# Attention with keys on partitions in a graph layer's twelve attention passes

## The chip, the cores and the metric

The kernel runs on one core of one Trainium2 chip. The metric is the device time in microseconds of one execution; the median of three runs is given. TensorE is written PE in the profile, VectorE DVE, ScalarE ACT, GpSimd POOL, SyncE SP.

## What is computed

A layer over 1250 nodes of 512 features: a graph convolution and a linear attention (not touched), then a block with three attentions of 8 heads, then an MLP. The three attentions are what the change is about:

```python
def attend(q, k, v):           # heads of 64 columns, 1250 tokens
    att = softmax(q @ k.T * 64 ** -0.5)
    return att @ v
spatial  = attend(xs @ Wq, xs @ Wk, xs @ Wv) @ Wo        # xs: one normed input
temporal = xt + attend_causal(xt @ Wq, ...) @ Wp         # keys after the query are masked
fused    = attend(spatial @ Cq, temporal @ Ck, temporal @ Cv) @ Co
```

Weights of the first two are those of an expert that a router picks. All is float32 in and out.

## The kernel before

Float32 products are made of two parts: hi (rounded to fp32r) and lo (the rest), and a product of three matmuls, hi by hi, hi by lo, lo by hi. The 8 heads of an attention are taken two at a time, so there are 12 passes (n = 0 to 11): 0 to 3 spatial, 4 to 7 temporal (causal), 8 to 11 the crossed one. In a pass two heads of 64 features lie on 128 partitions. The 1250 tokens are 10 tiles of 125 (TOK).

Steps of a pass, each written out in a list (STEPS, and lists for ScalarE and VectorE made from it):
- "u": q and k for both heads, features on partitions, 3 pieces of 418 columns each, 12 matmuls a piece (`unit`, L1892). ScalarE makes hi (L1124), VectorE lo (L1493).
- "v": values with tokens on partitions, 120 matmuls of 128 columns (`values`, L1930); ScalarE and VectorE write v_tok (L1163, L1549).
- "s": scores of one tile of queries against up to 500 keys, for the two heads in the two halves of the array (6 matmuls of 64 rows, L1951, L1959, L1961). VectorE takes them out of PSUM negated and scaled, with the row's minimum (L1516); ScalarE makes the exponential of a whole row and its sum (L1144), VectorE the reciprocal (L1529, one or two elements), GpSimd multiplies the whole row by it (L940).
- "t": a batch. Four 125x125 pieces of the probabilities are turned by TensorE (L1976); ScalarE rounds them to pt_hi (L1181), VectorE makes pt_lo (L1581).
- "p": 4 matmuls of 250 columns add the batch's part of the output to one bank (L1992). After the last batch of a unit (a pair of tiles and a head) ScalarE and VectorE write feat (L1152, L1539).

There are 50 batches in an unmasked pass and 30 in a causal one, 520 in all. The next pass's "u" and "v" stand near the end of a pass. In pass 1 a fold joins two weight matrices (`fold`, L1909). Between passes 7 and 8 GpSimd splits the planes of the temporal output and TensorE projects them (`project`, L2005), with a chain of VectorE and ScalarE behind each of the four projections (L1557, L1560, L1188, L1562). GpSimd also splits all weights into hi and lo (L848, L850); SyncE loads them in the order of use.

## Time and profile before

| what | value |
|---|---|
| median of 3 runs | 2180.38 us (2180.33 to 2619.19) |
| profiled execution | 2188.32 us |
| its span, first to last instruction | 2186.5 us |
| mean granted TensorE clock | 0.941 |
| TensorE, VectorE, ScalarE, GpSimd busy | 86%, 60%, 38%, 28% |
| attention stage, first "u" to last output | 515.4 to 1885.9 us |

Busy time is the union of an engine's instructions. TensorE's matmuls overlap in the profile, so what one costs is read from the distance of the starts, not from its duration. The granted clock is 1.0 at full speed and 0.5 at half.

### The profile page before, as it was taken

What the parts mean: (1) busy time and instruction counts of PE and PEld (TensorE: products, weight loads), DVE (VectorE), ACT (ScalarE), POOL (GpSimd) and SP (SyncE); (2) the same over time, 40 slices, a digit from 0 to 9 for tenths busy, and PEclk for the clock granted to TensorE, in tenths of its full rate; (3) what the DMA queues carried; (4) which work ended last, traced back from release to release, by engine and by line L of the source; (5) the groups of instructions that cost most, each with busy time, mean ns of one, the idle gap of its engine ahead of it and who ended that gap; (6) DMA issues with size and microseconds to landing.
All of it is one profiled execution on the core that took longest, in us unless ns stands there. A gap on an engine that the chain in (4) does not pass through costs nothing.

```text
span 2186.5 us, 35324 instructions
## 1 busy us (share of the span) xinstructions
PE 1885.5 (86%) x11839; PEld 1604.6 (73%) x11839; DVE 1302.4 (60%) x3667; ACT 828.7 (38%) x1490; POOL 602.7 (28%) x575
## 2 busy tenths in 40 slices
PE   1999999866898998989888887888989898876998
PEld 1687577655787886979777776777878786776886
DVE  6576577766676546575645546457676767552332
ACT  0223111022565545565544435246565655320000
POOL 2210011001324315141322213513231315546330
PEclk9999999957999998999989999899999999997999
DMA  3001000023000000020000000000000001002101
GB/s 97 30 6 44 6 25 15 1 104 119 15 1 25 20 30 15 18 92 1 16 1 15 11 6 16 18 6 12 1 16 1 16 1 72 29 28 68 39 29 47
DMA packets 24417, 60.83 MB, mean 28 GB/s; under 512 B 2522, under 2 KB 4790, under 8 KB 23373
## 3 DMA queue, kind: packets, MB, share of 16 engines
q1 hardware_dynamic: 24260, 58.74, 8.0%
q8 instruction: 98, 1.61, 0.3%
q14 instruction: 59, 0.48, 0.1%
HBM read 44.87 MB, written 13.86 MB: 27 GB/s over the span
## 4 chain that ended last, share of the span: by engine, by line
PE 56%; issue 14%; POOL 13%; DVE 10%; ACT 4%; DMA 1%; DVEq 1%; SPq 1%; POOLq 0%; ACTq 0%
PE ps L1892 7%; POOL probs L940 7%; PE ps L1992 7%; PE ps L2041 6%; PE ps L1976 6%; PE ps L1716 5%; PE ps L1930 4%; PE ps L1796 3%; PE ps L2070 3%; PE ps L1828 3%; PE ps L1951 3%; DVE probs L1516 2%; PE ps L1729 1%; DVE pt_lo L1581 1%; ACT pt_hi L1181 1%
## 5 line engine op out<-in xcount | busy, mean ns | idle before, releaser
L940 POOL TENSOR_SCALAR probs<-probs,stats 125x1250 f32<-125x1250 f32 (+4 forms) x240 | 280.8, 1180 | 926.0 <-DVE stats L1529 926.0
L1581 DVE TENSOR_TENSOR pt_lo<-ps,pt_hi 125x500 fp32r<-125x500 f32 x520 | 351.3, 677 | 186.2 <-ACT pt_hi L1181 181.2
L1181 ACT ACTIVATE pt_hi<-ps 125x500 fp32r<-125x500 f32 x520 | 304.8, 588 | 368.0 <-PE ps L1976 363.8
L1976 PE MATMUL ps<-ident,probs 125*125 125x125 f32 x2080 | 332.3, 286 | 87.3 <-POOL probs L940 87.3
L1992 PE MATMUL ps<-pt_hi,v_tok 125*128 125x250 f32 x1040 | 319.0, 328 | 55.5 <-DVE feat L1539 55.3
L1976 PEld LDWEIGHTS ps<-ident,probs 125*125 125x125 f32 x2080 | 285.7, 198 | 103.0 <-POOL probs L940 96.3
L1516 DVE TENSOR_SCALAR_CACHE_REDUCE probs<-ps 125x416 f32<-125x416 f32 (+5 forms) x624 | 340.6, 585 | 16.2 <-PE ps L1961 15.3
L1992 PEld LDWEIGHTS ps<-pt_hi,v_tok 125*128 125x128 f32 x1040 | 204.0, 196 | 139.4 <-DVE pt_lo L1581 77.5
L1144 ACT ACTIVATE probs<-probs,stats 125x1250 f32<-125x1250 f32 (+4 forms) x240 | 286.1, 1193 | 15.1 <-DVE stats L1521 15.1
L1992 PE MATMUL ps<-pt_lo,v_tok 125*128 125x250 f32 x1040 | 274.9, 286 | 0.0
L1992 PEld LDWEIGHTS ps<-pt_lo,v_tok 125*128 125x128 f32 x1040 | 205.5, 198 | 0.4
L1375 DVE TENSOR_SCALAR onehot<-iota_h,win_key,key_t 125x320 f16 x453 | 169.9, 375 | 0.5 <-issue 0.3
L1374 DVE TENSOR_SCALAR onehot<-iota_h,low_t 125x125 f16 x453 | 126.8, 280 | 61.8 <-PE ps L1828 31.8
L1951 PE MATMUL ps<-k_hi,q_hi 64*125 64x416 f32 (+5 forms) x624 | 146.9, 467 | 8.7 <-DVE k_lo L1493 5.8
L1930 PE MATMUL ps<-w_hi,xa_hi 128*125 128x128 f32 x480 | 131.3, 274 | 0.0
L1930 PE MATMUL ps<-w_lo,xa_hi 128*125 128x128 f32 x480 | 130.9, 273 | 0.0
L1930 PE MATMUL ps<-w_hi,xa_lo 128*125 128x128 f32 x480 | 130.8, 272 | 0.0
L1959 PE MATMUL ps<-k_hi,q_lo 64*125 64x416 f32 (+5 forms) x624 | 118.4, 375 | 0.0
L1961 PE MATMUL ps<-k_lo,q_hi 64*125 64x416 f32 (+5 forms) x624 | 114.7, 363 | 0.0
L1828 PE MATMUL ps<-onehot 125*125 x453 | 86.8, 312 | 17.8 <-DVE onehot L1375 17.3
L1796 PE MATMUL ps<-near_rows,adj 125*125 125x257 f32 (+1 forms) x400 | 94.5, 388 | 2.4 <-issue 2.1
L1951 PEld LDWEIGHTS ps<-k_hi,q_hi 64*125 64x125 f32 x624 | 59.8, 188 | 49.4 <-DVE k_lo L1493 7.6
(341 smaller groups left out, 3494.8 us busy)
## 6 DMA issues: line engine op xcount, KB each, us to landing
w_raw<-in_w_mlp SPq DMA_DIRECT2D x32, 256.0 KB, 2.6
w_raw<-in_w_gps SPq DMA_DIRECT2D x16, 256.0 KB, 2.6
w_raw<-in_w_tp SPq DMA_DIRECT2D x16, 256.0 KB, 2.6
w_raw<-in_w_sp SPq DMA_DIRECT2D x12, 256.0 KB, 5.4
w_raw<-in_w_cr SPq DMA_DIRECT2D x12, 256.0 KB, 2.6
d_xt<-xb_hi SPq DMA_DIRECT2D x1, 2508.0 KB, 9.3
d_xt<-xb_lo SPq DMA_DIRECT2D x1, 2508.0 KB, 14.9
xa_hi<-d_xt SPq DMA_DIRECT2D x1, 2508.0 KB, 9.6
```

The costliest lines, as they stand in the source:

```text
L940: pool.tensor_scalar(p, p, stats[:, slot, 7:8], 1.0, ALU.mult, ALU.mult).then_inc(s_prob, 1)
L1144: act.activation(p, p, ACT.Exp, scale=-1.0, bias=st[:, least:least + 1], accum_out=st[:, 4:5]).then_inc(s_exp, 1)
L1181: act.activation(pt_hi[:, (BASE_B[n] + m) % PT, :], ps[0:TOK, ring_bank(ring_of(n, m)), 0:4 * TOK], ACT.Copy)\
L1375: ins = dve.tensor_scalar(row[:, ET:ET + DH], iota_h[0:ET, :], win_key[0:ET, bass.ds(w, 1)], key, ALU.add, ALU.is_equal)
L1516: dve.tensor_scalar(probs[:, slot + h, first:first + w], ps[0:TOK, bank + h, 0:w], -SCALE, None, ALU.mult, ALU.min, accum_out=stats[:, slo ...
L1581: dve.tensor_tensor(pt_lo[:, slot, :], ps[0:TOK, ring_bank(ring_of(n, m)), 0:4 * TOK], f32(pt_hi[:, slot, :]), ALU.subtract).then_inc(s_pt ...
L1796: ins = pe.matmul(ps[0:TOK, bank + h, 0:257 - h], adj[t // 4][:, x, cols], near_rows[:, x, h, 0:257 - h], start=(x == 0), stop=(x == NT - 1))
L1892: ins = pe.matmul(ps[:, x % 4, 0:NP], w[:, k % 3, 128 * c:128 * c + 128], src[:, c, NP * p:NP * p + NP], start=(c == 0 and y == 0), stop=( ...
L1930: ins = pe.matmul(ps[0:TOK, ring_bank(r), 128 * t:128 * t + 128], x[:, c, (t0 + t) * TOK:(t0 + t + 1) * TOK], w[:, k % 3, 128 * c:128 * c ...
L1951: pe.matmul(ps[0:TOK, bank + h, 0:w], q_hi[r, tile], k_hi[r, first:first + w], start=True, stop=False)
L1976: ins = pe.transpose(ps[0:TOK, ring_bank(r), x * TOK:(x + 1) * TOK], probs[:, slot, kt * TOK:(kt + 1) * TOK], ident[0:TOK, 0:TOK])
L1992: ins = pe.matmul(ps[:, OUT_BANK, 0:2 * TOK], v_tok[:, kt, y % 2, :], part[:, slot, 2 * TOK * x:2 * TOK * (x + 1)], start=(kt == 0 and par ...
```

## The change

Scores are computed with keys on partitions and queries in the columns, so that the exponentials are already what the products need and nothing is turned. A step (n, i, h, b) is a pair of query tiles i, a head h and a pair of key tiles b; there are again 520. The parts:
- The row maximum must be known before. Approximate scores hi by hi are made in the old orientation, 64 rows, for both heads into banks 5 and 6 (task M), reduced by VectorE to a column, turned by TensorE (task R), and written negated by ScalarE into row 64 or 0 of q_row, whose partner in k_rest holds ones. The score matmul subtracts it.
- A score takes two matmuls of 250 columns for each key tile: k_both holds the head's hi on both halves, q_both has q's hi and lo; k_rest has k's lo and the ones, q_row q's hi and the row. Keys and queries are therefore written twice by ScalarE and in halves by VectorE.
- ScalarE writes the exponential to p_raw, GpSimd its fp32r part p_hi, VectorE p_lo.
- The values are linear like the keys, three pieces of 418 columns, and are turned by TensorE 64 columns at a time (task T). v_ones has the values' hi and 64 columns of ones, so that the products sum the probabilities too; a third matmul adds the values' lo part (v_rest): 6 matmuls in a step.
- At the end of a unit VectorE makes the reciprocal of the 64x250 sums and multiplies the output with it. Two output banks take turns.
- q is made in five pieces of 250 columns, in three ring slots. K, V, Q, M, R, T and the fold F are side tasks, put into steps by a planner with the costs in COST and a due step for each; each engine follows the same plan. Weights have a slot for each role; loads, splits and planes are put to steps too. Of the planes split between passes 7 and 8, two are split in pass 7 and the last by ScalarE and VectorE.

```diff
+STEP = [(n, i, h, b) for n in range(PASSES) for i in range(5) for h in range(2) for b in range(blocks_in(n, i))]
+STEP_NO = {s: g for g, s in enumerate(STEP)}
...
+COST = {"K": 2.3, "V": 2.3, "Q": 1.4, "M": 0.3, "R": 0.2, "T": 0.3, "F": 3.0}
...
+def tensor_steps():
+
+    steps = []
+    for first, end in ((0, FIRST[8, 0]), (FIRST[8, 0], len(STEP))):
+        if first:
+            steps.append(("J",))
+        steps += OPENING[STEP[first][0]] + [("S", first + x) for x in range(LEAD)]
+        for g in range(first, end):
+            if g + LEAD < end:
+                steps.append(("S", g + LEAD))
+            steps += SIDE[g] + [("P", g)]
...
+            def p_high(g):
+
+                pool.wait_ge(s_exp, g + 1)
+                if g >= PR:
+                    pool.wait_ge(s_pv, g - PR + 1)
+                pool.tensor_copy(p_hi[:, g % PR, :], p_raw[:, g % PR, :]).then_inc(s_p_hi, 1)
...
+            for g in range(LEAD):
+                p_high(g)
+            for g in range(len(STEP)):
+                if g + LEAD < len(STEP) and not FIRST[8, 0] - LEAD <= g < FIRST[8, 0]:
+                    p_high(g + LEAD)
...
+            def key_copy(n, p):
+
+                bias, b0 = BIAS[n // 4]
+                col, bank = b0 + n % 4, BANKS["K", n, p][0]
+                cols = slice(NP * p, NP * p + NP)
+                for h, r in enumerate(HALF):
+                    ins = act.activation(k_both[h][HALF[1 - h], n % 2, cols], ps[r, bank, 0:NP], ACT.Identity, bias=bias[r, col:col + 1])
+                ins.then_inc(s_k_both, 1)
...
+            def row_in(n, i):
+
+                bank = BANKS["R", n, i][0]
+                act.wait_ge(s_max_row, 5 * n + i + 1)
+                for h, r in ((0, 64), (1, 0)):
+                    ins = act.activation(q_row[h][r:r + 1, ring(n, i), :], ps[32 * h:32 * h + 1, bank, 0:2 * TOK], ACT.Copy, scale=-1.0)
+                ins.then_inc(s_max_in, 1)
...
+            def exponent(g):
+
+                act.wait_ge(s_score, g + 1)
+                if g >= PR:
+                    act.wait_ge(s_p_lo, g - PR + 1)
+                act.activation(p_raw[:, g % PR, :], ps[0:TOK, g % 3, 0:4 * TOK], ACT.Exp, scale=SCALE).then_inc(s_exp, 1)
...
-            def shift(n, u, j):
-
-                width, pieces = PLAN[n // 4][u]
-                if j == 0 and u >= 4:
-                    dve.wait_ge(s_pt, BASE_B[n] + last_batch(n, u // 2 * 2 - 3) + 1)
-                if j == 0 and u < 4 and n:
-                    dve.wait_ge(s_pt, BASE_B[n - 1] + last_batch(n - 1, u // 2 * 2 + 7) + 1)
-                bank, first, w = pieces[j]
-                dve.wait_ge(s_score, pieces_to(n, u) + j + 1)
-                slot = (20 * n + 2 * u) % PROBS
-                for h in range(2):
-                    dve.tensor_scalar(probs[:, slot + h, first:first + w], ps[0:TOK, bank + h, 0:w], -SCALE, None, ALU.mult,
-                                      ALU.min, accum_out=stats[:, slot + h, j:j + 1]).then_inc(s_taken, 1)
...
+            def maximum(n, i, y, j):
+
+                first, w = key_pieces(n, i)[j]
+                part = max_part[:, ring(n, i), :, :, :]
+                dve.wait_ge(s_max, MAX_NO["M", n, i, y, j])
+                dve.tensor_reduce(part[:, y, :, j], ps[0:TOK, 5:7, 0:w], AX.X, ALU.max).then_inc(s_max_part, 1)
...
+            def p_low(g):
+
+                dve.wait_ge(s_p_hi, g + 1)
+                if g >= PR:
+                    dve.wait_ge(s_pv, g - PR + 1)
+                dve.tensor_tensor(p_lo[:, g % PR, :], p_raw[:, g % PR, :], f32(p_hi[:, g % PR, :]), ALU.subtract).then_inc(s_p_lo, 1)
...
+            def unit_out(g):
+
+                n, i, h, _ = STEP[g]
+                u = unit_of(g)
+                dve.wait_ge(s_pv, g + 1)
+                dve.reciprocal(share[:, u % 2, :], ps[64:128, 3 + u % 2, 0:2 * TOK]).then_inc(s_share, 1)
+                dve.wait_ge(s_share, u + 1)
+                dve.tensor_tensor(feat[HALF[h], n % 4, 2 * TOK * i:2 * TOK * (i + 1)], ps[0:64, 3 + u % 2, 0:2 * TOK], share[:, u % 2, :],
+                                  ALU.mult).then_inc(s_o, 1)
...
+                for g in range(first, end):
+                    for what, *at in SIDE[g]:
+                        if what == "M":
+                            maximum(*at)
+                    if g > first and ends(g - 1):
+                        unit_out(g - 1)
+                    if g + LEAD < end:
+                        p_low(g + LEAD)
+                    if g > first:
+                        for task in SIDE[g - 1]:
+                            last_out(task)
+                    for what, *at in SIDE[g]:
+                        if what == "T":
+                            value_lo(*at)
...
+            def maximum(n, i, y, j):
+
+                first, w = key_pieces(n, i)[j]
+                tile = slice(TOK * y, TOK * y + TOK)
+                rows = [slice(ROW * h, ROW * h + ROW) for h in range(2)]
+                masked = CAUSAL[n // 4] and j == len(key_pieces(n, i)) - 1
+                left(("M", n, i, y, j))
+                pe.wait_ge(s_q_hi, 5 * n + i + 1)
+                pe.wait_ge(s_k_both, 3 * n + 3)
+                for h, r in enumerate(rows):
+                    ins = pe.matmul(ps[0:TOK, 5 + h, 0:w], q_both[h][r, ring(n, i), tile], k_both[h][r, n % 2, first:first + w],
+                                    start=True, stop=True)
...
+            def max_rows(n, i):
+
+                bank = BANKS["R", n, i][0]
+                left(("R", n, i))
+                pe.wait_ge(s_max_col, 5 * n + i + 1)
+                for y in range(2):
+                    ins = pe.transpose(ps[0:33, bank, TOK * y:TOK * y + TOK], max_col[:, ring(n, i), y, :], ident[0:TOK, 0:TOK])
+                ins.then_inc(s_max_row, 1)
...
+            def score(g):
+
+                n, i, h, b = STEP[g]
+                left(("S", g))
+                if h == 0 and b == 0:
+                    pe.wait_ge(s_max_in, 5 * n + i + 1)
+                    pe.wait_ge(s_q_lo, 5 * n + i + 1)
+                    if i == 0:
+                        pe.wait_ge(s_k_lo, 3 * n + 3)
+                if g == FIRST[4, 0]:
+                    pe.wait_ge(s_turned, 2)
+                rest = slice(0, 65) if h == 0 else slice(0, 128)
+                for x in range(2):
+                    tile = slice((2 * b + x) * TOK, (2 * b + x + 1) * TOK)
+                    to = ps[0:TOK, g % 3, 2 * TOK * x:2 * TOK * (x + 1)]
+                    pe.matmul(to, k_both[h][:, n % 2, tile], q_both[h][:, ring(n, i), :], start=True, stop=False)
+                    if CAUSAL[n // 4] and b == i:
+                        pe.matmul(to, identb[0:TOK, 0:TOK], mask_turned[0:TOK, TOK * (1 - x):TOK * (3 - x)], start=False, stop=False,
+                                  skip_group_check=True)
+                    ins = pe.matmul(to, k_rest[h][rest, n % 2, tile], q_row[h][rest, ring(n, i), :], start=False, stop=True)
...
-            def turned(n, m, y, b):
-
-                r = ring_of(n, m)
-                if b == 0:
-                    pe.wait_ge(s_prob, 20 * n + 4 * (y // 2) + y % 2 + 3)
-                if m < 3:
-                    pe.wait_ge(s_v_lo, 3 * n + m + 1)
-                else:
-                    pe.wait_ge(s_pt_lo, BASE_B[n] + m - 2)
-                for x in range(4):
-                    kt, u = 2 * b + x // 2, y // 2 * 2 + x % 2
-                    slot = (20 * n + 2 * u + y % 2) % PROBS
-                    ins = pe.transpose(ps[0:TOK, ring_bank(r), x * TOK:(x + 1) * TOK], probs[:, slot, kt * TOK:(kt + 1) * TOK],
-                                       ident[0:TOK, 0:TOK])
...
+            def product(g):
+
+                n, i, h, b = STEP[g]
+                bank = 3 + unit_of(g) % 2
+                pe.wait_ge(s_p_lo, g + 1)
+                left(("P", g))
+                for z in range(3):
+                    if first_use(n, h, z) == g or z == 1 and first_use(n, h, 1) == g:
+                        pe.wait_ge(s_turn_lo, TURN_NO["T", n, h, z])
                 for x in range(2):
-                    kt = 2 * b + x
-                    for part in (pt_hi, pt_lo):
-                        ins = pe.matmul(ps[:, OUT_BANK, 0:2 * TOK], v_tok[:, kt, y % 2, :],
-                                        part[:, slot, 2 * TOK * x:2 * TOK * (x + 1)],
-                                        start=(kt == 0 and part is pt_hi), stop=(kt == last and part is pt_lo))
+                    kt, cols, last = 2 * b + x, slice(2 * TOK * x, 2 * TOK * (x + 1)), b == blocks_in(n, i) - 1 and x == 1
+                    pe.matmul(ps[:, bank, 0:2 * TOK], v_ones[:, kt, h, :], p_hi[:, g % PR, cols], start=(b == 0 and x == 0), stop=False)
+                    pe.matmul(ps[:, bank, 0:2 * TOK], v_ones[:, kt, h, :], p_lo[:, g % PR, cols], start=False, stop=last)
+                    ins = pe.matmul(ps[0:64, bank, 0:2 * TOK], v_rest[:, kt, h, :], p_hi[:, g % PR, cols], start=False, stop=last,
+                                    skip_group_check=True)
```

## Rows read from the trace of the kernel before

**Rows 1.** The page: busy time of each engine, its share of the span, instructions

```profile
PE 1885.5 (86%) x11839; PEld 1604.6 (73%) x11839; DVE 1302.4 (60%) x3667; ACT 828.7 (38%) x1490; POOL 602.7 (28%) x575
```

**Rows 2.** Windows: busy time of each engine (instructions), TensorE's granted clock, DMA share, GB/s

```profile
515.40:1885.90 1370.50, 1211.16 (x8729) 1055.51 (x8730) 846.22 (x2334) 701.46 (x1276) 437.45 (x418) 0.95 0.06 21
515.40:556.10 40.70, 35.04 (x235) 32.16 (x235) 13.82 (x45) 9.38 (x18) 3.89 (x3) 0.92 0.37 147
668.50:805.50 137.00, 122.91 (x854) 106.32 (x852) 79.03 (x225) 67.02 (x118) 45.02 (x42) 0.95 0.10 30
1134.30:1229.40 95.10, 79.04 (x581) 69.57 (x581) 51.62 (x145) 44.51 (x92) 23.26 (x27) 0.93 0.03 9
1385.60:1458.40 72.80, 61.51 (x377) 57.22 (x376) 33.23 (x57) 14.06 (x22) 24.42 (x26) 0.99 0.05 15
1569.90:1681.40 111.50, 103.83 (x775) 90.15 (x773) 76.87 (x218) 64.16 (x114) 31.64 (x26) 0.98 0.03 8
```

**Rows 3.** Timeline of TensorE, one step of pass 8: start, us, instruction, count

```profile
1543.64 0.60 PE L1976 MATMUL ps<-ident,probs 125*125 125x125 f32 x4
1544.17 0.45 PE L1951 MATMUL ps<-k_hi,q_hi 64*125 64x418 f32 x2
...
1544.94 0.38 PE L1992 MATMUL ps<-pt_hi,v_tok 125*128 125x250 f32 x1
1545.16 0.28 PE L1992 MATMUL ps<-pt_lo,v_tok 125*128 125x250 f32 x1
...
1545.51 0.60 PE L1976 MATMUL ps<-ident,probs 125*125 125x125 f32 x4
```

**Rows 4.** Timeline of TensorE, inside a linear of keys, then of values

```profile
1539.24 0.35 PE L1892 MATMUL ps<-xa_lo,w_hi 128*128 128x418 f32 x1
1539.43 0.35 PE L1892 MATMUL ps<-xa_hi,w_lo 128*128 128x418 f32 x1
...
1560.58 0.27 PE L1930 MATMUL ps<-w_hi,xa_hi 128*125 128x128 f32 x1
1560.69 0.27 PE L1930 MATMUL ps<-w_lo,xa_hi 128*125 128x128 f32 x1
```

**Rows 5.** Waits of the whole span: who waited for whom, us, times, longest

```profile
PE ps L1976 <- POOL probs L940: 87.3, 39, 5.1
...
PE ps L1992 <- DVE feat L1539: 55.3, 72, 1.6
```

**Rows 6.** Lines by form, VectorE: busy us, mean ns, idle before

```profile
L1581 DVE TENSOR_TENSOR pt_lo<-ps,pt_hi 125x500 fp32r<-125x500 f32 x520 | 351.3, 677 | 186.2 <-ACT pt_hi L1181 181.2 <-issue 0.2
...
L1539 DVE SCALAR_TENSOR_TENSOR feat<-ps,tp_vecs,o_half 64x250 f32<-64x250 f32 x40 | 18.9, 473 | 43.9 <-ACT o_half L1152 43.4
...
L1549 DVE TENSOR_TENSOR v_tok<-ps,v_tok 125x256 fp32r<-125x256 f32 x48 | 17.8, 419 | 61.2 <-ACT v_tok L1163 61.1
...
L1493 DVE SCALAR_TENSOR_TENSOR k_lo<-ps,sp_vecs,k_hi 128x418 fp32r<-128x418 f32 x12 | 7.8, 653 | 19.7 <-ACT k_hi L1124 19.7
```

**Rows 7.** Lines by form, VectorE: a maximum and the two longest reciprocals

```profile
L1413 DVE TENSOR_REDUCE key_st<-mix_k 128x1 f32<-128x1250 f32 x4 | 5.8, 1455 | 13.8 <-ACT mix_k L1050 10.6 <-issue 2.1 <-ACT mix_v L1053 1.1
...
L1257 DVE RECIPROCAL ln_r<-ln_r 125x10 f32<-125x10 f32 x3 | 0.6, 216 | 2.2 <-ACT ln_r L1018 2.2
...
L1622 DVE RECIPROCAL end_r<-end_r 125x4 f32<-125x4 f32 x2 | 0.3, 160 | 0.0
```

**Rows 8.** Timeline: one subtraction of VectorE twice, and GpSimd beside the first

```profile
1418.86 1.85 DVE L1562 TENSOR_TENSOR xa_lo<-proj_tmp,xa_hi 128x1254 fp32r<-128x1254 f32 x1 [1.32 <-ACT xa_hi L1188]
...
1425.15 1.47 DVE L1562 TENSOR_TENSOR xa_lo<-proj_tmp,xa_hi 128x1254 fp32r<-128x1254 f32 x1 [1.31 <-ACT xa_hi L1188]
...
1418.09 1.30 POOL L850 TENSOR_TENSOR w_lo<-w_raw,w_hi 128x512 fp32r<-128x512 f32 x1
```

**Rows 9.** Lines by form, GpSimd's cast and ScalarE's reading of a 500-column bank

```profile
L848 POOL CAST w_hi<-w_raw 128x512 fp32r<-128x512 f32 x44 | 29.8, 678 | 108.9 <-DMA w_raw<-in_w_sp 43.3 <-PE ps L1729 29.6 <-DMA w_raw<-in_w_gps 23.6
...
L1181 ACT ACTIVATE pt_hi<-ps 125x500 fp32r<-125x500 f32 x520 | 304.8, 588 | 368.0 <-PE ps L1976 363.8
```

More of the change, by code:

```diff
@@ L1588, in _ @@
+                for task in SIDE[end - 1]:
+                    last_out(task)
+                unit_out(end - 1)
             for p in range(3):
@@ L1896, in fold @@
             def fold(x):
-                bank = (6 + x) % 4
+                bank = BANKS["F", x][0]
+                left(("F", x))
                 if x == 0:
```

1073 lines of the change are left out of this document (578 added, 495 removed).

## The prediction

> **What bounds the kernel now.** I read the page's busy shares first [rows 1]: TensorE is busy for 86% of the span, VectorE for 60%. Then the windows, with their edges at the first transposition (L1976) of a pass [rows 2]. The attention stage lasts 1370.5 us of the 2186.5, and TensorE is busy for 1211 of them, VectorE for 846. A pass without the causal mask takes 111.5 us (VectorE busy for 76.9), a causal one 95.1 (51.6), pass 1 with the fold 137.0, and from the end of pass 7 to the start of pass 8 72.8 go by.
>
> Pitches, not durations, give TensorE's cost, since its matmuls overlap. A product with 250 columns costs 0.117 us and the first after scores 0.22; four transpositions 0.53; three pairs of score matmuls 0.77, or 0.26 a pair [rows 3]. A linear with 418 columns costs 0.19, one with 128 columns 0.11 [rows 4]. An unmasked pass then holds 72 x 0.19 + 120 x 0.11 = 26.9 for q, k and v, 30 steps with scores of 1.87 (56.1) and 20 without, of 0.9 (1.87 less the scores and the 0.2 around them; 18): 101 us of work in 111.5. TensorE bounds these passes and gets 0.91 of the time. Its long waits are for the divided rows (87.3 us) and for the one output bank (55.3) [rows 5].
>
> **The change, TensorE.** It loses the 2080 transpositions of probabilities and two thirds of the 64-row score matmuls. Per unmasked pass after: k and v 72 x 0.19 = 13.7; q in 60 matmuls of 250 columns, 7.0; 20 turns of values and 10 of maxima at 0.11, 3.3; 30 pairs for the maxima at 0.26 and 0.1 for the row change behind each, 10.8; 50 steps of 4 score and 6 product matmuls, 500 x 0.117 = 58.5. Sum 93.3 against 101. The same sum for a causal pass (30 steps, 18 pairs, masks some 5) is 70.4. With 14 for the fold and 27 for the projection (144 x 0.19) TensorE has 8 x 93.3 + 4 x 70.4 + 41 = 1069 us.
>
> **The change, VectorE.** Here it adds more than it removes. 624 shifts with their minima go, 520 subtractions stay, and four things come.
> - The low part p_lo, 520 x 0.677 = 352 us [rows 6]. It now reads two tiles of SBUF.
> - The maxima. A reduction of 1250 elements took 1.455 us [rows 7]. A tensor_tensor grows by 1.06 ns per element (0.677 at 500, 0.419 at 256) [rows 6]; with 1.04 for a reduction, 833 elements in two banks cost 1.455 - 0.434 = 1.02. 240 unmasked pieces make 245 us. The 18 of a causal pass hold 15000 elements, 15.6 + 18 x 0.155 = 18.4, times four 74. With 60 short closing reductions at 0.16 (the shortest kind of row [rows 7]), 329.
> - The division of an output tile, 120 times a reciprocal of 64x250 and a product. The product is at most the 0.473 of today's last step over the same shape [rows 6], 0.45 taken. The reciprocal isn't shown at this size. From 4 to 10 elements it grows by 56 ns, 9.3 ns each [rows 7]; carried on, that is 0.216 + 240 x 0.0093 = 2.45 us. The low end, if only the part above a fixed 0.155 counts, is 6.1 ns each, 1.68. I take 2.1, between them: 120 x 2.55 = 306 us.
> - The halves of keys and queries: 72 x 0.653 + 120 x 0.473 = 104, and 72 low parts of values at about 0.38, 27 [rows 6].
>
> Sum 1118 us, 101.7 per unmasked pass and 75.9 per causal one. VectorE is above TensorE (93.3 and 70.4) in both, so the bound moves to it. The Trainium skill, VectorE: DVE Perf Modes, First, the fixed hardware budget, says that the reciprocal is an iterative divide with a repeat count of 8. At 0.96 GHz that would be an estimated 8.3 ns per element, 2.2 us for 250, and 12 us more in all than I count; the trace's 6.1 to 9.3 ns has it inside.
>
> **Its neighbours.** p_lo has two inputs in SBUF, and GpSimd reads SBUF beside it. The same kind of subtraction took 1.47 us alone and 1.85 with GpSimd's 1.30 us operation begun 0.77 us before it: it waited for the rest, some 0.4 [rows 8]. The Trainium skill, SBUF — State Buffer, Who interferes with whom, states this as an exclusive lock of a shared port; the trace agrees. GpSimd's new cast of 500 elements costs about 0.66 (0.678 for 512 [rows 9]), 520 times, beside the splits of weights. In a kernel that VectorE bounds, a cast starts about 2 us after the p_lo that let its products go (products 0.7, scores 0.47, the exponential, handovers), when the next p_lo is mostly over; I count only the splits, 30 us. If every p_lo met half a cast it would be 172.
>
> ScalarE: 50 exponentials at 0.59 and 51 short readings at up to 0.61 are at most 60 us per pass [rows 9], hidden. GpSimd: 33 for casts and some 11 for splits and planes, hidden. From a score to p_lo is 0.59 + 0.66 + 0.68 and three handovers, some 2.3 us; TensorE has two steps (at least 2.3, with side work 3.7) for it, so this loop doesn't bind. The two output banks take the wait of 55 us away; the wait for divided rows goes with the division on rows. The weights' DMAs move with the steps; a split stands some 12 steps (over 20 us) before its use, so SyncE's queue, in the same order, costs nothing; if that cover were gone, one late load would cost its few us, once.
>
> **Edges.** The opening drops from 40.7 us [rows 2] to about 28: six linears of 2.3 (12 x 0.19) and two of 1.4 are 16.6, and behind them run the last maximum, its turn, the row, the first score, exponential, cast and subtraction, with ScalarE's second copies in front, some 11. GpSimd's new memsets lie beside it. From pass 7 to 8: 3 us for the last plane, 9 until the first projection is complete, 25 of VectorE's chain of four projections, 28 of opening, 65 against 72.8. The last division adds 3 at the end. The extra time of the fold in pass 1 (137.0 against 111.5 [rows 2]) is in the stage's total of today; after, TensorE's 14 us lie under VectorE.
>
> **Sum.** VectorE's 1118 + 30, less some 32 that lie in the two openings, 1116. How well an engine in this chain of in-order lists is kept at work I take from today's bound, 0.91: 1226. With 28 + 65 + 3 the stage takes 1322 in place of 1370.5, 48.5 less. The span goes to 2138, the profiled execution (1.8 above its span) to 2140, and with its 8 us over the median, 2188.3 against 2180.4, the median to 2131.
>
> **Rivals.**
> - A: the reciprocal runs at one element per cycle at this size. For it: the 0.16 us of the small ones is all start-up. Against it: the 56 ns between 4 and 10 elements. VectorE falls by 120 x 1.65 = 198 to 920, TensorE bounds: (1069 - 67 for the projection and the openings) / 0.91 = 1101, plus 96; 173 less, 2007.
> - B, slower: lumps of the two engines don't hide each other. A linear holds TensorE for 2.3 us, and the maximum behind it in TensorE's list is first in VectorE's next step; a turn of values shares its bank with the next maximum, so VectorE waits one round (0.6) for it. With 132 linears at w and 72 turns at 0.6 in place of the 0.91, the stage is 96 + 1116 + 43 + 132 w; it passes today's from w = 0.9. At 1.7 (2.3 less a backlog of 0.6) it is 1479, and the time 2289. For it: 11 linears in 30 to 50 steps; against: the plan spaces them, and VectorE's division gives it a backlog.
> - C: p_lo meets a cast each time, 142 more, 156 with the 0.91, 2287. For it: the lock seen above. Against: the phase worked out above.
> - D: VectorE is kept at 0.97 of the time, since it does nothing else but wait for what is ready two steps ahead: 1116 / 0.97 + 96 = 1247, 124 less, 2056.
> - E: the new order starves at the short units at the start of a causal pass, so that these gain nothing and the forecast loses its 4 x 10 us: 2175.
>
> **How the numbers follow.** The forecast, with 0.88 to 0.95 of VectorE's time, 2080 to 2175: 0.40. A 0.13, B 0.18 (half of it between 2175 and 2225), C 0.06, D 0.15, E 0.08. The range reaches from A's time to the middle of B: 2005 to 2235. A measurement of this kernel tells 2% from no change. Faster than 2137: A, D and somewhat over half of the forecast, 0.51. Slower than 2224: half of B and most of C, 0.15. The same: 0.34.
>
> **What would show it.** VectorE's busy share in the stage should rise from 0.62 to 0.85 or more with TensorE's below it; the reciprocal's row should read 1.7 to 2.45 us; p_lo near 0.7 on the mean (1.0 for C); TensorE's main wait should be for p_lo. Rows of VectorE waiting for maxima, over 100 us, would be B. If VectorE is under 0.8 and TensorE too, the forecast's 0.91 is the step that failed.

## The result and the profile after

The changed kernel takes 2398.26 us (median of 4 runs, 2383.86 to 2409.42), the kernel before 2184.39 beside it: a ratio of 1.098, with 95% interval [1.090, 1.106]. One of the four runs of the kernel before was in a slow state (2619.19 us); ratios are of the means of the others. The forecast was 2131, with a range of 2005 to 2235.

The page of the kernel after, busy time of each engine, and the groups of its costliest new lines (columns as in [rows 1] and [rows 6]):

```profile
PE 1986.5 (83%) x11351; PEld 1694.8 (71%) x11351; DVE 1549.7 (65%) x2752; ACT 732.5 (31%) x1361; POOL 689.5 (29%) x856
...
L986 POOL CAST p_hi<-p_raw 125x500 fp32r<-125x500 f32 x520 | 346.1, 668 | 1019.6 <-ACT p_raw L1273 940.1
L1686 DVE TENSOR_TENSOR p_lo<-p_raw,p_hi 125x500 fp32r<-125x500 f32 x520 | 379.6, 735 | 182.9 <-POOL p_hi L986 179.5
...
L1662 DVE TENSOR_REDUCE max_part<-ps 125x2 f32<-125x832 f32 (+5 forms) x312 | 319.3, 1023 | 172.0 <-PE ps L2133 136.5
...
L2133 PE MATMUL ps<-k_both_a,q_both_a 64*125 64x416 f32 (+5 forms) x312 | 155.6, 499 | 125.0 <-DVE max_part L1662 89.0
L1693 DVE RECIPROCAL share<-ps 64x250 f32<-64x250 f32 x120 | 206.7, 1722 | 19.7 <-PE ps L2197 16.1
```

VectorE has 247 us more to do than in [rows 1]. The forecast had some 300 more (1118 + 30 against 846 in the stage), and the sizes of the single instructions are near its own: p_lo 0.735 us (0.677 and 30 us for the port were counted), a maximum 1.02, a cast 0.67, a reciprocal 1.72 (2.1 taken, 1.68 its low end). The time is lost elsewhere.

Windows of the kernel after: the attention stage, its first opening, then a causal pass, pass 7 with the projection and opening behind it, and passes 8 and 9. They answer to [rows 2]; the edges are the first product of a pass here, and the first transposition there.

```profile
513.20:2075.60 1562.40, 1308.66 (x8232) 1143.88 (x8232) 1089.80 (x1416) 602.67 (x1143) 513.33 (x690) 0.89 0.06 18
513.20:556.20 43.00, 35.71 (x156) 30.78 (x157) 17.25 (x28) 17.39 (x34) 10.86 (x12) 0.74 0.29 120
...
1218.70:1317.70 99.00, 82.20 (x559) 72.61 (x558) 71.38 (x96) 41.72 (x82) 25.47 (x36) 0.93 0.03 9
1413.70:1563.30 149.60, 116.82 (x671) 103.78 (x671) 102.02 (x114) 45.96 (x84) 52.04 (x64) 0.86 0.05 13
1563.30:1694.90 131.60, 114.84 (x737) 99.24 (x735) 98.75 (x129) 54.76 (x103) 41.62 (x57) 0.92 0.03 9
1694.90:1831.60 136.70, 114.72 (x711) 99.83 (x710) 95.03 (x127) 52.80 (x101) 38.35 (x56) 0.86 0.03 7
```

The stage takes 1562.4 us in place of 1370.5, 192 of the 195.6 us that the spans differ by. Passes 8 and 9 take 132 and 137 in place of 111.5 each, a causal pass 99.0 in place of 95.1. VectorE is busy for 1089.8 / 1562.4 = 0.70 of the stage, TensorE for 0.84. Neither is full. Pass 7 is no exception. In the kernel before, the 72.8 us of [rows 2] follow a short pass 7, which holds no linears of a next pass:

```profile
1324.70:1385.60 60.90, 47.82 (x340) 40.63 (x341) 37.27 (x100) 33.91 (x72) 25.98 (x33) 0.86 0.05 14
```

Together they are 60.9 + 72.8 = 133.7 us before, and 149.6 after.

Waits over the whole span (who waited for whom, us, times, longest):

```profile
DVE p_lo L1686 <- POOL p_hi L986: 179.5, 122, 5.9
...
DVE max_part L1662 <- PE ps L2133: 136.5, 95, 4.1
...
PE ps L2133 <- DVE max_part L1662: 89.0, 67, 3.0
...
PE ps L2159 <- DVE max_part L1662: 40.0, 28, 4.8
DVE max_part L1662 <- PE ps L2139: 32.6, 23, 4.8
...
PE ps L2195 <- DVE p_lo L1686: 20.1, 22, 1.9
```

The two engines wait for each other: VectorE 169 us (136.5 + 32.6) for the maxima's matmuls, TensorE 129 us (89.0 for the next maxima, 40.0 for turns of values) for a reduction that lets it write banks 5 and 6 again. The waits of [rows 5] (87.3 for the divided rows, 55.3 for the output bank) are gone, and these stand in their place.

To compare runs I split TensorE's stage into three parts. From its rows in the trace I take each distance from one start to the next, less the wait in it, sorted by line and by the granted clock. A line's mean distance at full clock, times its count, is its work; what the same matmuls took beyond that at a granted clock of 0.5 (1.2 GHz) is the surplus; the waits are the third part. The split is good to some 10 us. Before: 1163 + 48 + 159 = 1370. After: 1176 + 132 + 252 = 1560. **So the change takes no work off TensorE (13 us more), adds 93 us of waits, and 84 us come from time at the lower clock.** Why the clock is lower for longer isn't shown, since no run changes the clock alone.

### The profile page after: what moved, and what is told of

Same layout as the page of the kernel before. It is cut to its first block, busy times and chain, and to the rows that moved or that the text cites. A ratio compares the mean times of both kernels' runs of the same rounds, so it can differ in the third digit from the quotient of the medians.

```text
span 2382.1 us, 34620 instructions
## 1 busy us (share of the span) xinstructions
PE 1986.5 (83%) x11351; PEld 1694.8 (71%) x11351; DVE 1549.7 (65%) x2752; ACT 732.5 (31%) x1361; POOL 689.5 (29%) x856
## 4 chain that ended last, share of the span: by engine, by line
PE 59%; DVE 24%; issue 6%; POOL 4%; ACT 3%; DMA 1%; DVEq 1%; SPq 1%; POOLq 0%; ACTq 0%
PE ps L2075 11%; DVE max_part L1662 7%; PE ps L2250 6%; DVE p_lo L1686 5%; DVE share L1693 5%; PE ps L1889 5%; PE ps L2195 4%; PE ps L2133 4%; PE ps L1969 3%; PE ps L2197 3%; PE ps L2196 3%; PE ps L2279 3%; PE ps L2177 3%; PE ps L2181 3%; PE ps L2001 3%
## 5 line engine op out<-in xcount | busy, mean ns | idle before, releaser
L986 POOL CAST p_hi<-p_raw 125x500 fp32r<-125x500 f32 x520 | 346.1, 668 | 1019.6 <-ACT p_raw L1273 940.1
L1686 DVE TENSOR_TENSOR p_lo<-p_raw,p_hi 125x500 fp32r<-125x500 f32 x520 | 379.6, 735 | 182.9 <-POOL p_hi L986 179.5
L1273 ACT ACTIVATE p_raw<-ps 125x500 f32<-125x500 f32 x520 | 304.7, 587 | 462.5 <-PE ps L2181 456.4
L1662 DVE TENSOR_REDUCE max_part<-ps 125x2 f32<-125x832 f32 (+5 forms) x312 | 319.3, 1023 | 172.0 <-PE ps L2133 136.5
L2195 PE MATMUL ps<-p_hi,v_ones 125*128 125x250 f32 x1040 | 339.9, 327 | 21.1 <-DVE p_lo L1686 20.1
L2196 PE MATMUL ps<-p_lo,v_ones 125*128 125x250 f32 x1040 | 304.8, 293 | 0.0
L2197 PE MATMUL ps<-p_hi,v_rest 125*64 125x250 f32 x1040 | 304.5, 293 | 0.0
L2195 PEld LDWEIGHTS ps<-p_hi,v_ones 125*128 125x128 f32 x1040 | 209.9, 202 | 71.3 <-issue 34.0
L1693 DVE RECIPROCAL share<-ps 64x250 f32<-64x250 f32 x120 | 206.7, 1722 | 19.7 <-PE ps L2197 16.1
L2196 PEld LDWEIGHTS ps<-p_lo,v_ones 125*128 125x128 f32 x1040 | 214.6, 206 | 0.4
L2181 PE MATMUL ps<-q_row_a,k_rest_a 65*125 65x250 f32 x520 | 146.8, 301 | 0.0
L2181 PE MATMUL ps<-q_row_b,k_rest_b 128*125 128x250 f32 x520 | 146.4, 301 | 0.0
```

What stands on the lines that cost most here:

```text
L986: pool.tensor_copy(p_hi[:, g % PR, :], p_raw[:, g % PR, :]).then_inc(s_p_hi, 1)
L1273: act.activation(p_raw[:, g % PR, :], ps[0:TOK, g % 3, 0:4 * TOK], ACT.Exp, scale=SCALE).then_inc(s_exp, 1)
L1662: dve.tensor_reduce(part[:, y, :, j], ps[0:TOK, 5:7, 0:w], AX.X, ALU.max).then_inc(s_max_part, 1)
L1686: dve.tensor_tensor(p_lo[:, g % PR, :], p_raw[:, g % PR, :], f32(p_hi[:, g % PR, :]), ALU.subtract).then_inc(s_p_lo, 1)
L1693: dve.reciprocal(share[:, u % 2, :], ps[64:128, 3 + u % 2, 0:2 * TOK]).then_inc(s_share, 1)
L2181: ins = pe.matmul(to, k_rest[h][rest, n % 2, tile], q_row[h][rest, ring(n, i), :], start=False, stop=True)
```

## The experiments

All are edits of the kernel after, and all ratios are to the kernel before. Stage and parts (us) are those of the profiled run. nodiv leaves out the division; shortmax and tinymax leave out the search for the row maximum. These three don't compute the layer, and only price a part.

| run | us | ratio, 95% interval | stage | work + surplus + waits |
|---|---|---|---|---|
| before | 2180 to 2190 | 1 | 1370 | 1163 + 48 + 159 |
| after | 2398 | 1.098 [1.090, 1.106] | 1562 | 1176 + 132 + 252 |
| lead3 | 2395 | 1.094 [1.088, 1.099] | 1573 | 1172 + 157 + 242 |
| nodiv | 2318 | 1.059 [1.055, 1.063] | 1494 | 1175 + 123 + 195 |
| shortmax | 2232 | 1.020 [1.014, 1.026] | 1402 | 1168 + 72 + 160 |
| moved3 | 2359 | 1.078 [1.075, 1.082] | 1527 | 1173 + 129 + 221 |
| fullrows2 | 2428 | 1.111 [1.109, 1.114] | 1605 | 1165 + 137 + 300 |
| splitmax | 2416 | 1.106 [1.103, 1.109] | 1597 | 1210 + 163 + 222 |
| turn7 | 2471 | 1.132 [1.129, 1.135] | 1646 | 1164 + 193 + 286 |
| best2 | 2371 | 1.086 [1.083, 1.090] | 1547 | 1153 + 131 + 261 |
| halves | 2515 | 1.149 [1.143, 1.155] | 1700 | 1178 + 201 + 319 |
| halvesmoved | 2463 | 1.126 [1.120, 1.132] | 1626 | 1179 + 151 + 294 |
| mfirst | 2484 | 1.135 [1.129, 1.141] | 1662 | 1182 + 218 + 259 |
| tinymax | 2219 | 1.015 [1.009, 1.020] | 1389 | 1121 + 89 + 177 |
| ring3 | 2329 | 1.066 [1.063, 1.069] | 1508 | 1197 + 118 + 191 |
| aligned | 2370 | 1.086 [1.083, 1.090] | 1549 | 1178 + 144 + 224 |
| alignring | 2278 | 1.042 [1.039, 1.046] | 1458 | 1194 + 95 + 167 |
| alignringmoved | 2230 | 1.021 [1.018, 1.024] | 1409 | 1186 + 75 + 145 |
| best3 | 2232 | 1.018 [1.013, 1.023] | 1404 | 1182 + 84 + 135 |
| best4 | 2234 | 1.020 [1.016, 1.024] | 1400 | 1171 + 72 + 155 |

**Is it the amount of VectorE's work, or the depth of the pipeline?** (lead3, nodiv, shortmax, moved3)

```diff
 lead3:   -LEAD = 2; PR = 3     +LEAD = 3; PR = 4     (p_lo lies over p_raw)
 nodiv:   -dve.reciprocal(share[:, u % 2, :], ps[64:128, 3 + u % 2, 0:2 * TOK])
          +dve.tensor_scalar(share[:, u % 2, :], ps[64:128, ...], 0.0, 0.01, ALU.mult, ALU.add)
 shortmax:-dve.tensor_reduce(part[:, y, :, j], ps[0:TOK, 5:7, 0:w], AX.X, ALU.max)
          +dve.tensor_reduce(part[:, y, :, j], ps[0:TOK, 5:7, 0:2], AX.X, ALU.max)
          and ACT.Exp with scale=0.001
 moved3:  act.activation(p_hi, p_raw, ACT.Copy); pool.tensor_tensor(p_lo, p_raw, p_hi, subtract); as lead3
```

> The scores run three steps ahead of the products in place of two, with four slots for the probabilities; the exponential and its low part share a buffer (the low part is written over it) so that they fit. No work is added or removed. Lumps (a long side task of one engine starves the other because only two steps of work are ready between them): the waits of VectorE for p_hi (180 us in the changed kernel) fall below 80 us, the time falls by 50 to 120 us, to 2280 to 2350. Work (VectorE's amount of work sets the time, whatever the order): no change beyond 1%, 2375 to 2420. Shared banks (TensorE held at a maximum until VectorE has reduced the one before, 131 us for maxima and turns): those waits stay, the time falls by less than 40.

> The reciprocal of the 64x250 sums is replaced by a tensor_scalar of the same shape that writes a constant, so the division is left out: 120 times 1.72 us become about 0.41, 157 us less of VectorE's work, in one lump per unit. Work: the time falls by 157 or more (157 / 0.7 = 224 at the share of the stage in which VectorE is busy now), to 2175 to 2240. Lumps: the lump at the end of a unit is one of several, the time falls by 60 to 130, to 2270 to 2340. Clock (TensorE's stalls cost above all by the half clock behind them): the granted clock, 0.899 now, rises by the same share as the waits fall, and the fall is more than the removed waits of TensorE.

> The maxima are made over two columns of each bank in place of all, and the exponential's scale is 0.001 so that it stays finite: the search for the row maximum is left out, all matmuls stay. 312 reductions fall from 1.02 us to about 0.17, 265 us less of VectorE's work, and banks 5 and 6 are free 0.85 us earlier after each. Work: the time falls by 265 or more, to below 2130. Shared banks: TensorE's 131 us of waits for the maxima go nearly away and VectorE's for TensorE's maxima stay; with the smaller work 200 to 300 less. Lumps of the linears alone: under 120 less, since the linears of 2.3 us stay.

> ScalarE writes p_hi (a second activation, SBUF to SBUF, 500 elements, about 0.6 us), GpSimd makes p_lo (a two-input subtraction of 500 elements, about 1.27 us, alone), VectorE has neither: 380 us less of VectorE's work, ScalarE 300 more, GpSimd 310 more. With three steps ahead, as in the run beside it. Work of VectorE: the stage would be set by TensorE (93 us of work per unmasked pass) or by ScalarE (50 x 1.2 + 30 = 90): 8 x 103 + 4 x 80 + 96 = 1240 for the stage, the time 2060 to 2130, below the kernel before. Lumps: 2150 to 2280, with the waits of TensorE for p_lo growing, since the way from score to product is 2.9 us long.

VectorE's wait for p_hi in lead3, windows of the stage in nodiv and in shortmax, and three waits of moved3:

```profile
DVE p_lo L1687 <- POOL p_hi L987: 175.8, 120, 5.9
```

```profile
514.50:2008.80 1494.30, 1298.37 (x8232) 1136.84 (x8232) 945.47 (x1416) 603.36 (x1144) 508.04 (x688) 0.90 0.06 19
```

```profile
514.50:1916.70 1402.20, 1240.29 (x8232) 1092.33 (x8232) 833.48 (x1415) 603.44 (x1143) 516.26 (x689) 0.94 0.06 20
```

```profile
DVE max_part L1667 <- PE ps L2135: 314.7, 192, 6.3
...
PE ps L2135 <- DVE max_part L1667: 67.0, 51, 2.6
...
PE ps L2161 <- DVE max_part L1667: 37.8, 28, 3.2
```

The third step of lead changes nothing: the time stays, and so does VectorE's wait for p_hi, 176 us where the theory of lumps wanted under 80. Taking 144 us off VectorE by leaving out the reciprocal gives back 68 of the stage, 256 us off the reductions give 160, and 347 us of p_lo moved elsewhere give 36 (46 against lead3, which has the same lead). What a microsecond on VectorE is worth depends on where it stands: 0.6 in a reduction, 0.5 in a division, 0.1 in the low parts. With VectorE busy for half the stage (moved3), TensorE still waits 105 us for reductions. The amount isn't the bound; the reduction between two maxima is on the path. The expectations did worse than this reading: in time, nodiv's 80 us lie in the range for lumps, but shortmax's 166 and moved3's 39 lie in none of their ranges.

**Is it TensorE's row pairs, the pair of banks, or the turns in them?** (fullrows2, splitmax, turn7, best2)

```diff
 fullrows2: -ins = pe.matmul(..., q_both[h][r, ring(n, i), tile], k_both[h][r, n % 2, ...])
            +ins = pe.matmul(..., q_both[h][:, ring(n, i), tile], k_both[h][:, n % 2, ...])
 splitmax:  +for h in range(2): wait for s_max of this head; reduce ps[0:TOK, 5 + h, 0:w]; s_max_part + 1
            and TensorE waits for each head's bank by itself
 turn7:     -use = [5 + turn % 2]     +use = [7]     (for T and R, in steps without a linear;
            maxima two steps behind their queries)
 best2:     fullrows2, splitmax and turn7 together, and p_hi and p_lo moved as in moved3, at LEAD = 2
```

> Each product for the maxima is taken over all 128 rows of q_both and k_both (both heads in turn) in place of 64 rows for each head at once, and lies two steps behind its queries in place of one, since it now also reads their low parts. Theory that the switches between 64-row pairs and 128-row matmuls cost TensorE 0.2 us on either side: the two matmuls should take 2 x 0.17 to 0.19 us back to back and nothing around them, so 312 x about 0.2 = some 60 us of TensorE's work goes, the stage goes from 1562.8 to about 1500, and the time from 2384 to 2398 to about 2330. Rival, that TensorE only meets VectorE's maxima and the two shared banks: the same work is turned into longer waits for max_part (129 us in the kernel after would become 170 or more) and the time stays within 15 us.

> Each head's maxima are reduced by an instruction of their own and its bank is free from then on, so that TensorE can refill bank 5 while VectorE reads bank 6. Theory of the shared pair of banks: TensorE's waits for max_part (129 us in the kernel after) fall by half or more, the stage loses 40 to 60 us, less what 312 more starts on VectorE cost (312 x about 0.06 = 20 us of its work, which does not bound). Rival, switches of rows and the half clock alone: the waits move elsewhere (p_lo, q_both) and the stage stays within 15 us of 1562.8.

> The value turns and the turned maxima use the linears' bank 7, in steps that hold no linear, in place of taking turns on banks 5 and 6 with the maxima; maxima lie two steps behind their queries. Theory of the shared banks: the 40 us that turns wait for max_part in the kernel after go, and the part of the maxima's waits that stands behind a turn's two copies; the stage loses 30 to 60 us. Rival: the turns now wait for the linears' three readers in bank 7 and the linears for the turns' two, and the stage stays within 15 us or gets longer.

> All of it together: 128-row products for the maxima, one reduction per head, turns in bank 7, and the split's first part on ScalarE with its second on GpSimd, so that VectorE has 380 us less. If work (60 us), shared banks (50 to 90 us) and the half clock that follows the waits (up to 60 us) add up, the stage comes to about 1350 to 1400 us and the time to 2180 to 2230, about that of the kernel before. If one wait only takes the place of another, it stays above 2300 us, near the 2359 of the run that only moved the split.

All four miss what they were made for. turn7 (83 us of stage more) and best2 (2371 us) fall where their rivals put them, one wait in another's place; fullrows2 and splitmax got slower by 42 and 35 us of stage, which neither of their theories had. A wait of splitmax:

```profile
PE ps L2137 <- DVE max_part L1663: 65.4, 55, 2.7
```

Timeline of TensorE, a pair of 64-row matmuls for the maxima in the kernel after:

```profile
1609.64 0.28 PE L2177 MATMUL ps<-q_both_a,k_both_a 128*125 128x250 f32 x1
1609.76 0.28 PE L2181 MATMUL ps<-q_row_a,k_rest_a 65*125 65x250 f32 x1
1609.96 0.45 PE L2133 MATMUL ps<-k_both_a,q_both_a 64*125 64x418 f32 x1
1609.97 0.45 PE L2133 MATMUL ps<-k_both_b,q_both_b 64*125 64x418 f32 x1
1610.34 0.39 PE L2195 MATMUL ps<-p_hi,v_ones 125*128 125x250 f32 x1
1610.57 0.29 PE L2196 MATMUL ps<-p_lo,v_ones 125*128 125x250 f32 x1
```

and of fullrows2, with 128 rows, one without a wait and one behind a wait:

```profile
1608.12 0.28 PE L2180 MATMUL ps<-q_row_a,k_rest_a 65*125 65x250 f32 x1
1608.24 0.36 PE L2133 MATMUL ps<-k_both_a,q_both_a 128*125 128x418 f32 x1
1608.43 0.35 PE L2133 MATMUL ps<-k_both_b,q_both_b 128*125 128x418 f32 x1
1608.63 0.28 PE L2194 MATMUL ps<-p_hi,v_ones 125*128 125x250 f32 x1
...
1612.55 0.45 PE L2133 MATMUL ps<-k_both_a,q_both_a 128*125 128x416 f32 x1 [0.83 <-DVE max_part L1662]
1612.85 0.35 PE L2133 MATMUL ps<-k_both_b,q_both_b 128*125 128x416 f32 x1
```

Between 128-row neighbours at 0.117 us each, the 64-row pair delays the next matmul's start by 0.58 (1609.76 to 1610.34) and that one's follower by another 0.11: 0.69 less the 0.117 that the L2181 would have taken is 0.57 us, and the forecast counted 0.36. With full rows and no wait it is 0.39 for both heads, so in these two places full rows save 0.18. These are favourable places. The mean over all maxima between a score and a product, at full clock and without a marked wait, is 0.60 us in the kernel after (85 pairs) and 0.48 in fullrows2 (75). The sum of work in fullrows2 is only 11 us lower, though its masks also need 80 matmuls fewer: a matmul behind a wait lets its follower start 0.30 us later in place of 0.19 (1612.55), and the mean between the two heads is 0.25. The waits grew by 48: the full rows also read the queries' low parts, and come a step later. Splitting the reduction cut TensorE's waits for maxima's reductions, 89.0 to 65.4, and lost it in 34 us more of TensorE's work; my reading is the wait that now stands between the two halves of a pair. Turns in bank 7 wait for the linears' readers there (55 us at q_both alone).

**Are the linears' lumps the cause?** (halves, halvesmoved, mfirst, tinymax)

```diff
 halves:   +ahead = [("A", *task) for task in SIDE[g + 1] if task[0] in "KVQ"]   # its first 6 matmuls
           -steps += SIDE[g] + [("P", g)]     +steps += SIDE[g] + ahead + [("P", g)]
 halvesmoved: moved3 with this cut of the linears
 mfirst:   the step's M ahead of its ("S", g + LEAD) in TensorE's list
 tinymax:  as shortmax, and the unmasked maxima's matmuls with 2 columns
```

> Each linear of q, k and v outside the openings is cut in two: its first six matmuls go out at the end of the step before, its last six where the whole linear stood. The work is the same, but the longest block of TensorE between two maxima falls from 2.3 us to 1.15. Theory of lumps (the prediction's B: an engine that waits for the other's lump has no store of work, since the maxima have one pair of banks): VectorE's waits for the maxima's matmuls (169 us in the kernel after) and TensorE's for max_part (129 us) both fall, by a third or more, and the stage by 60 to 100 us, to a time of 2300 to 2340. Rival, TensorE's own work and the waits' fixed costs: the stage stays within 15 us of 1562, since not one matmul goes.

> The same cut with the low parts of the probabilities on GpSimd and their rounding on ScalarE, three steps ahead (the run moved3 with halved linears). Lumps of both engines are then at their shortest. Theory of lumps: 60 to 100 us under the 2359 of moved3, 2260 to 2300. Rival: within 15 us of 2359.

> TensorE's list has each step's maximum ahead of that step's scores in place of behind them, 0.47 us earlier. Theory of mutual waiting: VectorE's waits for the maxima's matmuls fall by up to 0.5 us each, TensorE's for max_part rise as much, and the stage changes by under 20 us. Theory that only VectorE's idle time counts: it falls by 50 us or more. If TensorE's waits alone count, it rises by 50 or more.

> As shortmax (reductions over 2 columns, a fixed small scale in the exponential, so the output isn't the reference's), and the unmasked maxima's matmuls have 2 columns in place of 416 or 418. It prices the columns of those 240 pairs. If TensorE's work bounds and a pair has about 0.2 us of column time in its 0.57, the stage loses 240 x (0.17 to 0.25) = 40 to 60 us against shortmax's 1402, to a time of 2170 to 2190, no better than the kernel before even with the maxima nearly free. If the pairs' columns ran beside other work or in waiting time, it stays within 15 us of 2232.

Waits of halves:

```profile
DVE max_part L1669 <- PE ps L2151: 268.9, 142, 7.3
...
PE ps L2082 <- DVE q_both_b L1651: 92.6, 31, 5.1
...
PE ps L2151 <- DVE max_part L1669: 69.7, 50, 3.0
...
PE ps L2082 <- DVE k_rest_b L1640: 40.9, 19, 4.2
```

Halved linears ask for bank 7 a step earlier, and TensorE waits 134 us for VectorE's last reading of the linear before (37 in the kernel after). The edit brought a wait of its own, so it says nothing of lumps; halvesmoved has the same wait (117 us) and lies 104 us above moved3, where 60 to 100 less were hoped for. Its use is another: such a wait stands in TensorE's list ahead of all maxima, and VectorE's waiting for them went from 169 to 307 us. mfirst moved waiting from VectorE's maxima (169 to 114) to its low parts (180 to 324), and lost 99 us: the scores, one after the maximum now, stand behind its wait. TensorE's waits alone hardly grew, 252 to 259; 86 of the 99 us are surplus at the lower clock. None of the three theories had that in it, though the sign is the third's. tinymax takes 47 us of work from TensorE and wins 13 in the stage (its rival's "within 15"), since 17 come back as waits and 17 as surplus. TensorE's work alone isn't the bound either. What is left is the row of reductions, one after another, that both lists pass through; the next four runs test it.

**Give the maxima a store, and let the lumps meet.** (ring3, aligned, alignring, alignringmoved)

```diff
 ring3:    -use = [entry[1] % 3]   (scores)     +use = [entry[1] % 2]
           -use = [5, 6]           (maxima)     +use = [(2, 5, 6)[(turn + x) % 3] for x in range(2)]
           with one reduction for each head, as splitmax
 aligned:  +if task[0] in "KVQ" and STEP[g][3] and (n >= 8 or n < 3) and DUE[task] > g - 1: continue
 alignring:      both
 alignringmoved: both, and p_hi and p_lo moved as in moved3, at LEAD = 2
```

> The scores use two banks in place of three (the exponential of a step is over long before the scores two steps on), and the maxima, one bank and one reduction per head as in splitmax, and the turns go round three banks. Theory of the missing store (a maximum can't be issued until VectorE has reduced the one before it): TensorE's waits for max_part (129 us in the kernel after) nearly go, VectorE finds a maximum ready more often, and the stage falls by 70 us or more under splitmax's 1597 and under the 1562 of the kernel after. Rival, in-order lists alone set the meeting points: the waits move to other names and the stage stays within 20 us of splitmax.

> The plan lets the linears of q, k and v of the passes 0 to 2 and 8 to 11 stand only in steps that begin a unit, where VectorE divides the unit before (82 of 132 linears beside a division, in place of 37); nothing else is changed. Theory of lumps (TensorE's 2.3 us and VectorE's 2.13 us are paid one after the other where they don't meet): in these passes some 6 more linears per pass lie beside a division, 6 x up to 2.1 = 6 to 13 us a pass, 35 to 75 us in six passes; passes 8 to 10 fall from 132 to 150 us to 125 to 135. Rival, the meeting points don't depend on the lumps: within 15 us of the kernel after.

> Both edits together. If the store and the lumps are the same loss, the sum is less than the two effects; if they are separate, they add: 1562 less 105 to 150. If neither is the cause, 1562 to 1600.

> Both edits and the low parts of the probabilities on GpSimd, their rounding on ScalarE (VectorE 380 us less), two steps ahead. If what is left is TensorE's own 1165 to 1180 us of work with the waits and half clock that the kernel before also had (160 and 50), the stage comes to 1390 and the time to 2200, level with before. If the meetings still set the time, 2300 or more.

The lumps, in the timeline of the kernel after: a division on VectorE, and a linear of TensorE behind it.

```profile
1603.27 1.71 DVE L1693 RECIPROCAL share<-ps 64x250 f32<-64x250 f32 x1
...
1604.77 0.45 PE L2133 MATMUL ps<-k_both_a,q_both_a 64*125 64x416 f32 x1
...
1605.02 0.41 DVE L1695 TENSOR_TENSOR feat<-ps,share 64x250 f32<-64x250 f32 x1
1605.16 0.45 PE L2075 MATMUL ps<-xa_hi,w_hi 128*128 128x418 f32 x1
1605.35 1.25 DVE L1686 TENSOR_TENSOR p_lo<-p_raw,p_hi 125x500 fp32r<-125x500 f32 x2
...
1606.53 1.01 DVE L1662 TENSOR_REDUCE max_part<-ps 125x2 f32<-125x832 f32 x1
...
1607.46 0.66 DVE L1686 TENSOR_TENSOR p_lo<-p_raw,p_hi 125x500 fp32r<-125x500 f32 x1
```

The maximum issued at 1604.77 is reduced only at 1606.53, behind the division, its product and two low parts, and ends at 1607.54. Had TensorE wanted its next maximum in the meantime, it would have stood still; here a linear (1605.16 to 1607.5) lies just beside. `aligned` makes this the rule in seven passes: the linears that stand in the first step of a unit, where VectorE divides the unit before, go from 37 of 132 to 82, with no other edit. It wins 13 us of the stage and 28 of the time. By the stage that is within the 15 us of its rival, and under the 35 of its theory; the intervals of the two ratios, up to 1.0897 and from 1.0903, lie barely apart. So by itself it shows little. ring3, with the same reductions as splitmax, is 89 us of stage and 87 us of time below it (69 of time below the kernel after). The two differ only in the banks, and the third bank of maxima and turns comes from the scores: this is what moving one bank is worth. Together they win 104 of the stage and 120 of the time, more than their sum of 67 and 97. My reading, not tested by itself, is that with a store the lumps that lie side by side are hidden, and that without one even those are met by a maximum. Waits of ring3 and of alignring:

```profile
DVE max_part L1669 <- PE ps L2145: 90.8, 64, 4.6
...
PE ps L2145 <- DVE max_part L1669: 62.5, 62, 3.2
```

```profile
DVE max_part L1671 <- PE ps L2147: 71.8, 63, 4.4
...
PE ps L2147 <- DVE max_part L1671: 36.9, 56, 2.0
```

TensorE's 129 us of waiting for reductions, the turns' share in it, went to 62 with one bank more and to 37 with both edits, and VectorE's 169 for maxima to 95 with both. Moving the low parts off VectorE now gives 48 us. The stage and a wait of alignringmoved:

```profile
514.50:1923.20 1408.70, 1261.62 (x8232) 1107.05 (x8232) 756.66 (x1207) 909.72 (x1663) 794.48 (x688) 0.93 0.06 20
```

```profile
PE ps L2148 <- DVE max_part L1675: 18.7, 26, 1.4
```

**What is left?** (best3, best4)

```diff
 best3:  alignringmoved with LEAD = 3, PR = 4, p_lo over p_raw
 best4:  best3 with one wait for both banks ahead of a pair of maxima's matmuls
```

> alignringmoved with the scores three steps ahead and p_lo written over p_raw. TensorE's waits for p_lo (21 us) should go, and with them some time at half clock: 20 to 40 us less than 2230, 2190 to 2210. If what is left is TensorE's own work at about 1186 us, it can't pass the kernel before: its floor is that work plus the openings and the projection that both kernels have. A rival that lets it pass: the waits for max_part, max_col and p_lo go together, 2150.

> best3 with one wait ahead of a maximum's two 64-row matmuls in place of one before each, so that they start together again. The decomposition gave splitmax and ring3 20 us more of TensorE's work than the kernel after (1197 to 1210 against 1176), put down to the wait between the two. If that is right, it is 10 to 20 us faster than best3; if the second bank's freedom was worth more, it is slower.

Both stay at the level of alignringmoved, where 20 to 40 us less were expected of best3, and 10 to 20 more of best4. In best3 waits and surplus are 219 us, 12 more than the 207 of the kernel before, and TensorE's work is 1182 against 1163. In best4 the single wait takes 11 us off the work, and 20 come back in waits, both near what the split can tell. No version here beats the kernel before.

## Why the prediction was wrong

The step that failed is the share of 0.91 for which VectorE was to be kept at work: it was busy for 0.70 of the stage, and waited 169 us for maxima. Ahead of it, the sum for TensorE was 107 us short, so that TensorE and not VectorE has the more work.

- **What bounds before.** TensorE's 101 us of work in a pass of 111.5: the distances between 1569.9 and 1681.4 us give 102.4 at full clock. Right, for this pass.
- **TensorE after, the first step that failed.** 1069 us were summed, 1176 measured. The term of the maxima, 0.26 + 0.1 for a pair, is 0.57 in the timeline above: 312 x 0.21 = 66 us (75 by the mean of 0.60). The 0.26 came from three pairs in a row [rows 3], where no pair stands alone between 128-row matmuls; the sum of today had counted 0.2 around such a row, the sum of after only 0.1. Linears at 0.166 us a matmul in place of 0.19 and 0.117 by kind add 15, turns at 0.154 in place of 0.11 add 11; 15 us I can't assign. With the right sum, the change takes nothing from TensorE, and the bound doesn't move to VectorE: 1176 us of work against 1090.
- **VectorE after.** 1118 + 30 summed, 1090 measured. The low parts with the port 382 against 379.6, the maxima 329 against 319 and their closings, the division 306 against 206.7 and 120 x 0.41 = 256. Right, with the reciprocal at the low end of its bounds. The 8 repeats that the Trainium skill gives it (VectorE: DVE Perf Modes, First, the fixed hardware budget) would be an estimated 8.3 ns an element; the row reads 6.9, so the measurement decides against that estimate here.
- **"How well an engine in this chain is kept at work I take from today's bound, 0.91", the step that decided.** VectorE came to 0.70. Two things were wrong with it. It was read from one unmasked pass: by the same distances TensorE had 74 of the 95.1 us in the causal pass from 1134.3, 0.78, and 1163 / 1370 = 0.85 over the stage. By 0.85 the forecast's own sum is 1116 / 0.85 + 96 = 1409 us of stage (an estimate), 38 more than today's. The measured 1562 asks for 1116 / (1562 - 96) = 0.76. For that part the runs show the store: 0.91 belonged to a TensorE whose products run two steps behind the scores, so it has work in hand; the maxima have one pair of banks and no store, and each reduction stands between two matmuls of theirs. A third bank and lumps side by side gave back 120 us of the time, and the shortened reductions 166.
- **Rival B** named this mechanism and its sign, over 100 us of VectorE waiting for maxima: 169. It had 0.18, and its 2289 was 109 us short: it priced the linears and turns, and neither the surplus at the lower clock nor TensorE's missing 107 us. Its linears beside the maxima are not the whole of it: aligned alone gave 28 us. A (0.13), C and D are out: reciprocal 1.72, p_lo 0.735, VectorE not full. E was half right: the causal passes gained nothing (99.0 against 95.1), but no other pass did either.
- **"So this loop doesn't bind".** lead3 bears it out: the time stays within 0.2%.
- **Edges.** The opening took 43.0 in place of 28, at a granted clock of 0.74.
- **The signs.** TensorE's main wait should have been for p_lo; it is 20 us, and 129 for max_part. "If VectorE is under 0.8 and TensorE too" is met for VectorE (0.70) and not by TensorE's busy share (0.84), which holds the surplus; its work alone is 1176 / 1562 = 0.75.
- **What stays open.** With the store, the lumps and the low parts mended, the stage is still 38 us longer than before (1409), and the surplus at the lower clock has been measured and not explained.

## What to carry to other kernels

When a new step makes an engine's result the licence for another engine's next instruction (write, reduce, write again in the same bank), price the round trip, not either engine's sum; the share of time for which an engine is kept at work today was measured on a chain with its own store, and needn't hold for a chain without one. Before adding engines or moving work, look for one more buffer in that loop, and lay the long blocks of the two engines beside each other. Take today's share over every kind of pass, not over the best one. And price a kind of instruction by its distance to the neighbours that it will have.

## What the runs showed of the hardware

- A pair of 64-row matmuls with 418 columns costs 0.57 us between 128-row matmuls, though both run at once for 0.45 and three such pairs in a row cost 0.26 each [rows 3]; two 128-row matmuls of that width cost 0.39 there. The means are 0.60 and 0.48.
- A reciprocal of 64x250 from PSUM takes 1.72 us, 6.9 ns per column, against 0.41 for a product of that shape.
- In these runs more waiting goes with more time at 1.2 GHz: 145 us of waits in the stage with 75 us of surplus, 252 with 132, 319 with 201. The scatter is large (222 with 163, 300 with 137).
